# LayerNorm 1's row statistics of chunks 4 to 15 computed on VectorE instead of ScalarE

## What is computed

```python
def _layernorm(x, axis=-1, eps=1e-05):
    m = jnp.mean(x, axis=axis, keepdims=True)
    v = jnp.var(x, axis=axis, keepdims=True)
    return (x - m) / jnp.sqrt(v + eps)
...
h = _layernorm(x) * (1 + ca) + sa              # LayerNorm 1
x = x + ga * attn(h)      # omega, zeta, F by matmul; a recurrence over the 2048 tokens; y = xs @ C.T + h @ D.T
h = _layernorm(x) * (1 + cb) + sb              # LayerNorm 2
x = x + gb * ffn(h)       # token shift, k = xk @ Wk, r = sigmoid(xr @ Wr), out = r * (relu(k)**2 @ Wv)
```

## Time and profile before

| | us |
|---|---|
| median of 3 executions | 1021.52 |
| lowest and highest | 1020.16, 1022.26 |
| the profiled execution, its own time | 1023.01 |
| its span, first to last instruction | 1021.2 |
| TensorE busy (PE) | 951.0 (93%) |
| VectorE busy (DVE) | 787.3 (77%) |
| ScalarE busy (ACT) | 753.7 (74%) |
| GpSimd busy (POOL) | 100.8 (10%) |
| mean granted TensorE clock | 0.974 |

### The profile page before, as it was taken

The page is one execution under the profiler, slowest core; times in us unless marked ns, Lnnn a source line. Parts: engine busy times, 40 slices in busy tenths (PEclk is TensorE's granted clock), DMA queues, the critical chain, the costliest instruction groups (busy, mean ns, idle before and its releaser), DMA issues.

```text
span 1021.2 us, 14942 instructions
## 1 busy us (share of the span) xinstructions
PE 951.0 (93%) x5072; PEld 813.0 (80%) x5072; DVE 787.3 (77%) x2161; ACT 753.7 (74%) x1571; POOL 100.8 (10%) x117
## 2 busy tenths in 40 slices
PE   6898888889999998999999998999999998999997
PEld 6577767778788887888878887888878887888786
DVE  2788668877786987888796987888788877797563
ACT  2787788688778778888778788878778797755551
POOL 0001000120111111010101002010101002000000
PEclk9987988999999999999999999999999999999999
DMA  8740202021121202121121202111120211111001
GB/s 280 248 125 1 84 19 84 1 82 42 56 81 42 78 24 76 42 83 42 42 93 39 74 24 84 42 54 71 42 94 19 65 52 42 42 42 42 22 21 42
DMA packets 35276, 64.79 MB, mean 63 GB/s; under 512 B 3704, under 2 KB 4344, under 8 KB 35200
## 3 DMA queue, kind: packets, MB, share of 16 engines
q1 hardware_dynamic: 35200, 63.84, 18.7%
HBM read 47.02 MB, written 16.81 MB: 63 GB/s over the span
## 4 chain that ended last, share of the span: by engine, by line
PE 81%; DVE 7%; ACT 6%; issue 4%; DMA 1%; POOL 0%; SPq 0%; DVEq 0%; ACTq 0%
PE ps_kr L318 31%; PE ps_cd L318 19%; PE ps_tv L318 17%; PE ps_pt L318 7%; PE ps_tv L359 2%; PE ps_pt L326 2%; PE ps_tv L369 2%; ACT mix_full L699 1%; DVE mix_full L943 1%; ACT square_out L560 1%; DMA x<-in_wmod 1%; ACT x_in L550 0%; DVE tmp L1147 0%; DMA gate_rows<-kk 0%; DVE h_lo L874 0%
## 5 line engine op out<-in xcount | busy, mean ns | idle before, releaser
L943 DVE SCALAR_TENSOR_TENSOR mix_full<-ps_tv,cur_m,mix_full 128x256 f32<-128x256 f32 x256 | 120.2, 478 | 105.1 <-ACT mix_full L699 104.6
L699 ACT ACTIVATE mix_full<-ps_tv,cur_m 128x255 f32<-128x255 f32 x256 | 119.6, 573 | 6.0 <-PE ps_tv L359 6.0
L1411 POOL TENSOR_SCALAR var<-sq 128x2 f32<-128x2 f32 (+1 forms) x47 | 32.5, 691 | 858.1 <-ACT square_out L560 858.1
L721 ACT ACTIVATE kk<-ps_kr 128x512 f32<-128x512 f32 x64 | 36.6, 590 | 103.1 <-PE ps_kr L318 103.1
L318 PE MATMUL ps_tv<-wv_hi,kk_hi 128*128 128x512 f32 x256 | 73.4, 410 | 27.4 <-issue 27.4
L318 PE MATMUL ps_kr<-mix_k_hi,wk_hi 128*128 128x256 f32 x512 | 81.8, 283 | 8.1 <-issue 8.1
L318 PEld LDWEIGHTS ps_tv<-wv_hi,kk_hi 128*128 128x128 f32 x256 | 49.2, 197 | 40.6 <-issue 29.0
L318 PE MATMUL ps_kr<-mix_k_lo,wk_hi 128*128 128x256 f32 x512 | 81.1, 281 | 0.0
L318 PEld LDWEIGHTS ps_kr<-mix_k_hi,wk_hi 128*128 128x128 f32 x512 | 71.9, 192 | 11.1 <-issue 8.7
L318 PE MATMUL ps_kr<-mix_k_hi,wk_lo 128*128 128x256 f32 x512 | 80.7, 280 | 0.0
L578 ACT ACTIVATE x_in<-x_in,norm_bias,rstd 128x512 f32<-128x512 f32 x62 | 45.5, 807 | 45.8 <-POOL norm_bias L1418 43.2
(11 more groups left out here) (201 smaller groups left out, 2310.6 us busy)
## 6 DMA issues: line engine op xcount, KB each, us to landing
x<-in_x SPq DMA_DIRECT2D x32, 512.0 KB, 3.6
out<-x SPq DMA_DIRECT2D x32, 512.0 KB, 2.8
x_in<-in_x SPq DMA_DIRECT2D x15, 1024.0 KB, 5.2
x<-in_wmod SPq DMA_DIRECT2D x3, 1024.0 KB, 7.8
mix_full<-in_wmod SPq DMA_DIRECT2D x2, 1024.0 KB, 6.8
x_in<-in_x SPq DMA_DIRECT2D x2, 512.0 KB, 5.3
stage_out<-in_wd SPq DMA_DIRECT2D x1, 1024.0 KB, 8.0
stage_mix<-in_wk SPq DMA_DIRECT2D x1, 1024.0 KB, 9.0
```

Source lines behind the costliest of these rows:

```text
L699: mm = act.activation(mix[n][:, k, 1:UNIT], ps_tv[:, j, c * UNIT:(c + 1) * UNIT - 1], ACT.Identity, bias=cur_m[:, SHIFT + k:SHIFT + k + 1] ...
L721: act.activation(kk[:, i, :], ps_kr[:, i, :], ACT.Relu).then_inc(s_relu, 1)
L943: dve.scalar_tensor_tensor(mix[n][:, k, :], ps_tv[:, j, c * UNIT:(c + 1) * UNIT], cur_m[:, alpha + k:alpha + k + 1], mix[n][:, k, :], ALU. ...
L1411: pool.tensor_scalar(var[:, :], sq[:, :], 1.0 / D, EPS, ALU.mult, ALU.add).then_inc(s_var, 1)
```

## The change

On ScalarE the calls of `sums1(q + 3)` and `squares1(q + 3)` leave the even slot; `normalise1(q + 3)` stays where it was. On VectorE a new step `statistics1(q + 3)` runs in the even slot, behind `residual(u + 2)` and three recurrence steps and ahead of `read_out(u)`: four `bn_stats`, four `bn_aggr` and one `tensor_scalar`. On GpSimd `rstd1_of` takes the variance from `bn` for every chunk but 1 to 3, and `norm_bias1` waits for the negated mean as well. Chunks 1 to 3 keep ScalarE's two passes.

```diff
@@ -842,14 +842,11 @@
                         mix_high(u + 1, 1)
                     if q + 2 < NCHUNK:
                         softplus_parts(q + 2)
-                    if next_t1:
-                        sums1(q + 3)
                     if q + 2 < NCHUNK:
                         squared_angle(q + 2)
                     if next_cd:
                         statistics2(u + 2)
                     if next_t1:
-                        squares1(q + 3)
                         normalise1(q + 3)
                 else:
                     relu_squared(u)
@@ -970,6 +967,23 @@
                     dve.tensor_scalar(xn2[:, i, :], x2[:, u % 4, i, :], neg_mean2[:, u % 2, i:i + 1],
                                       rstd2[:, u % 2, i:i + 1], ALU.add, ALU.mult).then_inc(s_xn2, 1)
                     yield
+
+            def statistics1(q):
+
+                dve.wait_ge(s_xin, q * 16)
+
+                dve.wait_ge(s_norm_bias1, q)
+                done = (q - 3) * TPC
+                for i in range(TPC):
+                    dve.bn_stats(bn_parts[:, i, :], x_in[:, i, :]).then_inc(s_bn, 1)
+                    yield
+                for i in range(TPC):
+                    dve.wait_ge(s_bn, done + i + 1)
+                    dve.bn_aggr(bn[:, i, :], bn_parts[:, i, :]).then_inc(s_sq1, 1)
+                    yield
+                dve.wait_ge(s_sq1, q * TPC + TPC)
+                dve.tensor_scalar(neg_mean1[:, :], bn[:, :, 0], -1.0, None, ALU.mult).then_inc(s_mean1, 1)
+                yield
 
             def gated_tanh(u):
 
@@ -1375,6 +1389,8 @@
                     if next_cd:
                         run(residual(u + 2))
                         take(rec, 3)
+                    if next_t1:
+                        run(statistics1(q + 3))
                     beside(rec, read_out(u), 2)
                     if next_cd:
                         beside(rec, normalise2(u + 2), 1)
@@ -1413,8 +1429,15 @@
                 pool.tensor_tensor(rstd[:, :], var[:, :], minus_half[:, 0:n], ALU.pow).then_inc(s_rstd, 1)
 
             def rstd1_of(q):
-                rstd_of(sq1, var1, rstd1, q, s_sq1, s_var1, s_rstd1)
+                if 1 <= q <= 3:
+                    rstd_of(sq1, var1, rstd1, q, s_sq1, s_var1, s_rstd1)
+                else:
+                    pool.wait_ge(s_sq1, q * TPC + TPC)
+                    pool.tensor_scalar(var1[:, :], bn[:, :, 1], 1.0, EPS, ALU.mult, ALU.add).then_inc(s_var1, 1)
+                    pool.wait_ge(s_var1, q + 1)
+                    pool.tensor_tensor(rstd1[:, :], var1[:, :], minus_half[:, :], ALU.pow).then_inc(s_rstd1, 1)
                 pool.wait_ge(s_rstd1, q + 1)
+                pool.wait_ge(s_mean1, q + 1)
                 pool.tensor_tensor(norm_bias1[:, :], neg_mean1[:, :], rstd1[:, :], ALU.mult).then_inc(s_norm_bias1, 1)
 
             def rstd2_of(u):
@@ -1422,13 +1445,7 @@
 
             pool.memset(minus_half[:, :], -0.5).then_inc(s_pool_const, 1)
             pool.wait_ge(s_pool_const, 1)
-            pool.wait_ge(s_sq1, TPC)
-            pool.tensor_scalar(var1[:, :], bn[:, :, 1], 1.0, EPS, ALU.mult, ALU.add).then_inc(s_var1, 1)
-            pool.wait_ge(s_var1, 1)
-            pool.tensor_tensor(rstd1[:, :], var1[:, :], minus_half[:, :], ALU.pow).then_inc(s_rstd1, 1)
-            pool.wait_ge(s_rstd1, 1)
-            pool.wait_ge(s_mean1, 1)
-            pool.tensor_tensor(norm_bias1[:, :], neg_mean1[:, :], rstd1[:, :], ALU.mult).then_inc(s_norm_bias1, 1)
+            rstd1_of(0)
             rstd1_of(1)
             rstd2_of(0)
             rstd2_of(1)
```

## The result

| | before | changed |
|---|---|---|
| median, us | 1020.88 (4 runs) | 1009.74 (4 runs) |
| lowest and highest | 1020.16, 1022.26 | 1007.73, 1011.79 |
| profiled execution, own time | 1023.01 | 1010.76 |
| its span | 1021.2 | 1009.0 |
| mean granted clock | 0.974 | 0.984 |

The ratio is 0.989, 95% interval 0.986 to 0.992. The change makes the kernel 11 us faster in these runs; 1014.0 was forecast, with 1009 to 1027 around it.

The account below looks back on a forecast made before the run. Bound: TensorE's work plus twelve gaps (26.5 us) ahead of v_product, set by the chain statistics, GpSimd, normalise1, shifted, mixes, kk_lo. 1023.01 less 3.6 (gaps) and 4.5 (clock) gives 1014.9; 1014.0 taken; 8-in-10 range 1009 to 1027, own 1010 to 1020.

Parts of the forecast that it names:

- The first pass brings nothing: ScalarE's sums: removing them gains nothing, as ScalarE still sits idle behind them for 1.44 us until x2 is ready.
- The added work, 2.89 us: VectorE, from where read_out started: bn_stats, bn_aggr and tensor_scalar take 2.40 + 0.40 + 0.09 = 2.89 us per pair.
- The rival of whole durations: VectorE's added instructions cost their whole durations, 3.3 us instead of 2.89; time 1019 us; chance 0.03.
- GpSimd's three steps, 1.57 us: GpSimd's LayerNorm 1 steps take 1.57 us instead of 2.89 or 3.90, norm_bias reading 0.1 us ahead of second read_out's end.
- the signs: Listed profile evidence, including ScalarE waiting longer than 3.02 us for norm_bias, though that wait ends 0.9 us earlier.
- The reason given, any two SBUF operands: GpSimd is held while VectorE streams two SBUF operands, or one through normalise2; read_out takes one operand from PSUM.
- the first rival: GpSimd's norm_bias misses the second read_out and is held; v_product 0.9 or 1.9 us later, 17.8 us, 1039 us; chance 0.20.
- The new gap, 1.82 us and 3.55 in the first pair: TensorE, mid odd slot: transposes wait for the later normalise2, 1.82 us in eleven pairs and 3.55 in the first.
- The sum of the gaps, -3.6 us: TensorE: old gaps of 27.2 us (26.5 + 0.66) replaced by 11 x 1.82 + 3.55 = 23.6, net -3.6 us.
- The clock, -4.5 us: TensorE: three of the four v_products slowed by a lower clock behind gaps recover, 3 x 1.5 = -4.5 us.
- the clock behind every new gap: TensorE's clock falls behind all twelve new gaps: 11 x 1.5 us on top, 1030 us; chance 0.03.
- GpSimd as slow as before: GpSimd's steps stay slow wherever they stand: v_product 0.43 us later, 12 x 0.43 = +5 us, 1027 us; chance 0.07.

Follow-up runs that it names:

- run 1: Kernel before, without ScalarE's first pass (row sums) for chunks 4 to 15, an old sum used instead: 1017.87 us, ratio 0.9996.
- run 5: Changed kernel with two of the four bn_stats left out for chunks 4 to 15: 998.25 us, ratio 0.979.
- run 2: Changed kernel with the four recurrence steps moved ahead of both read_outs on VectorE, in the slots of chunks 4 to 15: 1009.08 us, ratio 0.9934.
- run 10: Changed kernel with one spare power on GpSimd between rstd1 and norm_bias1, its tile allocated last: 1013.47 us, ratio 0.9960.
- run 11: Changed kernel with two spare powers on GpSimd between rstd1 and norm_bias1, their tile allocated last: 1043.71 us, ratio 1.0252.
- run 9: Changed kernel with an unused tile of 48 bytes a partition ahead of bn_parts, no instruction differing: 1016.7 us, ratio 0.9983.
- run 12: Changed kernel with three spare 128x4 products on GpSimd ahead of its wait for LayerNorm 1's variance, tile allocated last: 1010.75 us, ratio 0.9926.
- run 3: Changed kernel with statistics1 behind normalise2 instead of ahead of read_out: 1066.75 us, ratio 1.050.
- Run 6: Kernel before with one spare power on GpSimd between rstd1 and norm_bias1, its tile moving those behind it: 1047.82 us, ratio 1.028.

## Why the prediction was right, and where not

The forecast of 1014.0 was 4 us too high. The measured 1009.74 lies in the range of 8 in 10, and 0.3 us outside the own range of 1010 to 1020.

- **The first pass brings nothing**: held (run 1).
- **The added work, 2.89 us**: 2.85, in order and parts as worked out. The rival of whole durations fell. Half of the `bn_stats` taken away took the gap down with it (run 5).
- **GpSimd's three steps, 1.57 us**: held to the hundredth in all twelve pairs, and the second `read_out` was met with 0.15 us to spare. ScalarE's wait for `norm_bias` grew from 3.02 to 4.82 us, as named among the signs. The step was called the weakest, and that was wrong twice. Short steps behind `read_out` do not hold a power that starts beside them (run 2), and `norm_bias` may come 1 us later before `v_product` feels it (run 10). The reason given, any two SBUF operands, does not carry: the rival that rested on it was given 0.20 and had less in its favour. A hold by the unbroken row further on is real (run 11). The prediction also miscounted this row before the change: the power takes 1.40 us in six pairs and 3.27 in six, not five and seven (the first pair has 1.40 and yet a gap of 2.58 us), which makes the first rival's 17.8 us 16.8.
- **The new gap, 1.82 us and 3.55 in the first pair**: 1.81 to 1.90 from start to start; 3.50 idle in the first pair.
- **The sum of the gaps, -3.6 us: this is the term that was mis-sized; it was -6.4.** The new gaps were worked out as a delay of a start (end of `normalise2` to start of the transposes), the old ones taken as idle time from the chain of waits, 26.5 us. These are two measures. An idle time leaves out the overlap that is lost with it: from start to start the old gaps cost 29.5 us, 0.24 more each and 2.9 in all. The new ones came to 23.1, where the forecast's were 11 x 1.82 + 3.55 - 0.66 = 22.9 on top of what the first pair had.
- **The clock, -4.5 us**: -4.2 in the two profiles, one drop left in the first pair, as forecast. But as a step from one profile to another it is luck: run 1 had the old gaps and no drop, and this term was over half of the forecast's gain. What the change does to it can be said only as a chance: before, seven gaps of 2.5 us or more in which a drop may come, after it one. The medians, with drops mixed in on both sides, differ by 11.1 us.
- The rest of the distance from 1014.9 to 1010.76 in the profiled executions is 1.6 us ahead of the first pair. It is no effect of the change: run 5 has 3.6 us more there than the changed kernel, with the same instructions. With the 2.8 of the gaps and 0.3 less of the clock that is 4.1, as measured.

The rivals of the clock behind every new gap (1030) and of GpSimd as slow as before (1027) both fell by the changed kernel's own profile.

## What to carry to other kernels

Measure gaps in one way, from start to start of the engine that sets the end; idle times in the listing were 0.15 to 0.24 us shorter than what they cost. When a step moves to another engine, look for its place by when its input is there and by what is queued behind it there: the same work brought 8 to 11 us behind the gating, and 31 us in the idle times ahead of it with GpSimd's and ScalarE's steps moved forward too. And give a spare tile in an experiment its place behind all others, or the addresses become part of the experiment.

## What the runs showed of the hardware

- **Addresses.** A shift of most SBUF tiles by 48 bytes a partition lengthened `k_product` from 5.47 to 5.75 us and `cd_product` from 6.84 to 6.99, and the kernel by 6 us (run 9 against run 12). The products with `mix_r` and `wv` became up to 0.06 us shorter. Which tile's place matters, and what offset would serve it, was not tried.
- **The clock behind a gap.** "Slow" is a `v_product` whose granted clock averages 0.65 to 0.80 instead of 1.00, so that a part of it ran at the lower level. Behind 2.5 to 2.65 us without work it was slow four times in seven in the kernel before and never in seven in run 1. Behind 2.49 to 2.83 us it was slow three times in seven in run 11, and not behind the three longest of these. Behind 2.93 to 2.97 us it was slow nineteen times in nineteen (runs 3 and 6), but there the transposes ahead of the gap also took 1.1 to 1.3 us instead of 1.04. Run 6 has it behind one of two gaps of 2.15 us and one of three of 2.42. Behind 1.5 to 1.83 us it never came in ten (the kernel before and run 1), nor behind the eleven gaps of 1.65 to 1.74 at L359. A slow one took 1.3 to 1.6 us longer, in run 3 up to 2.8. So the length of the gap alone does not decide; what else does was not found.
- **GpSimd beside VectorE.** A 128x4 step took 0.20 us beside `bn_stats` and 1.76 to 2.04 us in eight pairs of run 11, in a row of steps most of which read two SBUF operands, past several changes of instruction. In the other four pairs of the same run it was done after 0.68 us, during L1068, which reads one. What decides at which change GpSimd is let in stays open.
